# Issuing the query side's three spreads of keys and queries from ScalarE's queue instead of SyncE's

## What is computed

```python
# 64 samples of x and ctx (64 x 256 each); two samples make one pair
x = x + L0_xattn(layernorm(x), ctx)      # 8 heads of 8 channels, rotary positions on q and k:
    # q, k, v = Wq x + bq, Wk c + bk, Wv c + bv ;  q, k = rotary(q), rotary(k)
    # scores = q k^T / sqrt(8) ; p = softmax(scores) ; out = Wo (p v) + bo      (scores 256 x 256 a head)
x = x + L0_ffn(layernorm(x))             # three ternary linears, 256 -> 1024 -> 256, silu gate
x = x + L1_xattn(layernorm(x), ctx)      # one head over 64 memory rows, masked
x = x + L1_ffn(layernorm(x))             # bf16 ternary weights, silu gate, rms norm, 256 -> 1024 -> 256
```

## Time and profile before

| | us |
|---|---|
| median of 3 runs | 884.59 (882.81 to 884.67) |
| the profiled execution's own time | 885.19 |
| its span, first to last instruction | 883.4 |
| DVE busy | 744.9 (84%) |
| PE busy | 766.2 (87%) |
| ACT busy | 688.0 (78%) |
| POOL busy | 659.1 (75%) |

### The profile page before, as it was taken

One profiled execution on the slowest core, in us unless ns is written; L12 is line 12 of the kernel. 1 busy time (PEld: TensorE's weight loads), 2 busy tenths in 40 slices (PEclk: granted clock), 3 DMA queues, 4 the chain that ended last, 5 costly groups with the idle time before them and its releaser, 6 DMA issues. The chain is left out here.

```text
span 883.4 us, 21920 instructions
## 1 busy us (share of the span) xinstructions
PE 766.2 (87%) x6804; PEld 407.7 (46%) x6804; DVE 744.9 (84%) x1707; ACT 688.0 (78%) x1469; POOL 659.1 (75%) x1115
## 2 busy tenths in 40 slices
PE   0037878899999999999999999999999999998745
PEld 0023333444555555555555555555555554444422
DVE  0765778889999999999999999999999999966731
ACT  3655667779888888888888888888888889895531
POOL 5664435668888888888888888888888887677652
PEclk9995788889999999999999999999999999998986
DMA  9101122224444444444344444544444443345212
GB/s 338 11 13 55 38 64 57 78 72 103 104 109 108 104 109 104 101 114 103 101 101 104 107 109 109 110 107 105 109 109 105 104 102 98 90 85 108 68 46 71
DMA packets 210859, 84.67 MB, mean 96 GB/s; under 512 B 152748, under 2 KB 209708, under 8 KB 210744
## 3 DMA queue, kind: packets, MB, share of 16 engines
q1 hardware_dynamic: 210744, 83.28, 37.9%
HBM read 28.42 MB, written 4.72 MB: 38 GB/s over the span
## 5 line engine op out<-in xcount | busy, mean ns | idle before, releaser
L871 DVE TENSOR_REDUCE mx<-psS 128x2 f32<-128x512 f32 x512 | 338.2, 680 | 22.1 <-PE psS L435 21.4
L591 ACT ACTIVATE prob<-psT 128x512 f32<-128x512 f32 x512 | 293.8, 603 | 33.6 <-PE psT L443 32.6
L435 PE MATMUL psS<-KQ 31*128 31x256 f16 x1024 | 142.7, 283 | 23.5 <-DVE mx L871 21.5
L522 PE MATMUL psW<-guT,xT 128*128 128x512 bf16 x512 | 132.1, 393 | 15.8 <-DMA xT<-stage 13.1
L457 PE MATMUL psW<-prob,vst 128*32 128x256 f32 x2048 | 135.2, 394 | 0.1
L443 PE MATMUL psT<-KQ 32*128 32x256 f16 x1024 | 134.1, 278 | 1.0 <-ACT prob L591 0.5
L435 PEld LDWEIGHTS psS<-KQ 31*128 31x128 f16 x1024 | 42.1, 93 | 112.9 <-DVE mx L871 65.7
L777 POOL TENSOR_TENSOR stage<-stage 128x512 f16<-128x512 f32 x64 | 73.2, 1162 | 17.7 <-ACT stage L674 17.5
L457 PEld LDWEIGHTS psW<-prob,vst 128*32 128x32 f32 x2048 | 55.5, 111 | 60.5 <-issue 23.8
L484 PE MATMUL psW<-tern,xqT 128*128 128x512 bf16 x256 | 77.8, 386 | 4.0 <-DMA xqT<-xqB 3.6
L522 PEld LDWEIGHTS psW<-guT,xT 128*128 128x128 f16 x512 | 44.0, 100 | 76.9 <-issue 37.0
(11 more groups left out here) (163 smaller groups left out, 1772.8 us busy)
## 6 DMA issues: line engine op xcount, KB each, us to landing
KQ<-hl SPq DMA_DIRECT2D x192, 64.0 KB, 2.0
xP<-in_x SPq DMA_DIRECT2D x32, 128.0 KB, 2.2
cP<-in_ctx SPq DMA_DIRECT2D x32, 128.0 KB, 2.2
xA<-in_x SPq DMA_DIRECT2D x32, 128.0 KB, 2.5
oV<-uA SPq DMA_DIRECT2D x32, 128.0 KB, 2.2
oR<-rden_d SPq DMA_DIRECT2D x128, 32.0 KB
cB<-in_ctx SPq DMA_DIRECT2D x32, 128.0 KB, 2.3
out<-x SPq DMA_DIRECT2D x32, 128.0 KB, 1.8
```

Of the source, the lines that this page charges most:

```text
L435: m = nc.tensor.matmul(psS[:, n % 2, T * k:T * k + T], KQ[p % DEEP][r, 1, g, 128 * k:128 * k + 128], KQ[p % DEEP][r, 0, g, :], start=True, ...
L522: m = nc.tensor.matmul(bank, xT[:, NK * part + k, :], w[:, k, :], start=(k == 0 and part == 0), stop=(k == NK - 1 and part == 1))
L591: m = nc.scalar.activation(flat(prob[:, n % 8, :, :]), psT[:, n % 2, :], ACT.Exp, scale=float(HC) ** -0.5)
L871: m = nc.vector.tensor_reduce(mx[:, p % 2, :, 4 * (n % 4) + n // 4], psS[:, n % 2, :].rearrange("p (c s) -> p c s", c=NK), AX.X, ALU.max)
```

## The change

In ACT's row of `ORDER` a new step `kqa:1` stands behind `c1`, that is in the steady stretch behind `E10` and `pc` and ahead of `E11`. It issues the three transfers of the queries' side from ACT's queue; `kq` on SP keeps the three of the keys' side. Each has its own semaphore, and whoever waited for six transfers on `kq` waits for three on each. The sources, destinations, sizes and everything else are the same.

```diff
     "act": """...
-           E10:-1 pc:2 c1:28 E11:-1 tc4:1 E12:-1 mn:0 ...
+           E10:-1 pc:2 c1:28 kqa:1 E11:-1 tc4:1 E12:-1 mn:0 ...
@@ sp
                     elif name == "kq":
                         after_apart(sp, "lo", p)
                         after_apart(sp, "T", p - DEEP)
-                        for r, (k, q) in enumerate(((1, 2), (1, 3), (0, 2))):
-                            for side, part in enumerate((k, q)):
-                                sp.dma_start(KQ[p % DEEP][r::4, side, :, :], hl[:, part, :]).then_inc(S["kq"], 16)
+                        for r, part in enumerate((1, 1, 0)):
+                            sp.dma_start(KQ[p % DEEP][r::4, 0, :, :], hl[:, part, :]).then_inc(S["kq"], 16)
@@ pe, step S0
-                            after_dma(pe, "kq", p, 6)
+                            after_dma(pe, "kq", p, 3)
+                            after_dma(pe, "kqa", p, 3)
@@ act
+                    if kind == "kqa":
+                        after(act, "lo", p)
+                        after(act, "T", p - DEEP, NH - 1)
+                        for r, part in enumerate((2, 3, 2)):
+                            nc.scalar.dma_start(KQ[p % DEEP][r::4, 1, :, :], hl[:, part, :]).then_inc(S["kqa"], 16)
+                        continue
@@ act, step hi; the same on pool, step lo
-                        after_dma(act, "kq", p - 1, 6)
+                        after_dma(act, "kq", p - 1, 3)
+                        after_dma(act, "kqa", p - 1, 3)
```

More of the change, by code:

```diff
@@ L79 @@
     "act": """pTc:-5 xr:-3 hh1:-6 ab2:20 rn0:24 tc5:-4 E6:-1 E7:-1 xq:-3 sq0:-6 fr0:13 tc2:6 c0:37 E8:-1 u0:-1 E9:-1
-           E10:-1 pc:2 c1:28 E11:-1 tc4:1 E12:-1 mn:0 xh:-5 tB0:-3 tB1:-3 x1:-2 ab1:22 tc0:16 E13:-1 mxc:0 rn2:20
+           E10:-1 pc:2 c1:28 kqa:1 E11:-1 tc4:1 E12:-1 mn:0 xh:-5 tB0:-3 tB1:-3 x1:-2 ab1:22 tc0:16 E13:-1 mxc:0 rn2:20
            E14:-1 E15:-1 sq1:-6 hi:2 u1:-1 vst:2 E0:0 E1:0 th0:-5 xcTc:-4 tc1:8 E2:0 fr1:2 fr2:1 hr0:-3 E3:0 hr1:-3
@@ L771, in body @@
                         after(pool, "hi", p)
-                        after_dma(pool, "kq", p - 1, 6)
+                        after_dma(pool, "kq", p - 1, 3)
+                        after_dma(pool, "kqa", p - 1, 3)
                         m = nc.gpsimd.tensor_tensor(hl[:, 0::3, :], rot[:], hl[:, 1:3, :], ALU.subtract)
```

## The result

The changed kernel takes 909.39 us (median of 4 runs, 908.76 to 910.4) beside 884.63 us for the kernel before: the ratio is 1.0286, with a 95% interval of 1.0268 to 1.0303. It is 25 us slower, and outside the predicted range. The profiled execution took 909.59 us, 907.8 of it span.

What follows compares the result with a forecast made beforehand. DVE was taken as the bound, busy 21.94 of 22.60 us a period. From the profiled 885.19 us, -0.8 (start) + 0 + 0 gave 884.4, stated as 883.8 us against the median 884.59; range 881.0 to 894.

Steps and rivals of the forecast that it cites:

- What bounds the kernel: Steady period of 22.60 us: DVE is the bound, busy 21.94 us; ACT has 2.6 us of slack.
- SP's three issues: SP, steady stretch: losing three issues a pair frees 1.8 us, but nobody waits for SP, so the gain is 0.
- the place named for harm: ACT behind `pc`: late issues would delay `E11`, then `tB0` and `tB1`, then the second `aB` on DVE.
- The step that failed: ACT's steady stretch: its queue reads ahead by four or more, so three issues end by 411.1 or 411.6; cost 0.
- ends: ACT's three issues: cost 0 if its queue reads far ahead, 17 to 26 us if they start only after `pc`.
- Rival B: ACT's queue holds one instruction behind the running one, so part of the issue shows: 885 to 892 us, chance 0.17.
- The lateness absorbed: Between `E11` and the second `aB` on DVE: a lateness of 0.5 us is absorbed, DVE loses the rest.
- The 0.38 us wait before `x2`: DVE's wait for PE, 0.38 us a period: part of a lateness comes back there, since PE can catch up.
- -0.8: Start, `S0` of pair 0: earlier landing of transfers gains between 0 and 1.66 us; the middle, -0.8, was taken.
- rival C: The issue stops ACT, starting only after `pc`, and delays `S0` at the start by 1.6 us: 903 to 912, chance 0.15.
- the case in which both queues issue at once: Start, pair 0: ACT issues three beside SP's, the last landing at 71.95, so the whole 1.66 us wait goes.
- Rival D: Steady stretch: earlier transfers shorten the period itself, where DVE idles before `x2`: about 880.5 to 882.5 us, chance 0.10.

Runs made afterwards that it cites:

- The version from pair 7 on: The changed kernel, but pairs 0 to 6 have all six transfers on SP and `kqa` issues only from pair 7 on: 897.35 us, ratio 1.0145.
- `kqa` behind `E8`: The changed kernel with ACT's three issues behind `E8`, ahead of `u0`, instead of behind `pc`: 893.58 us, ratio 1.0118.
- `T10` ahead of `pc`: The changed kernel with ACT's three issues one place earlier, directly ahead of `pc` instead of behind it: 910.89 us, ratio 1.0302.
- `T3` behind `hr1`: The kernel before, all six transfers on SP, plus three idle issues on ACT behind `hr1` into a tile nobody reads: 890.64 us, ratio 1.0078.
- `E11` 2.07 us late: The changed kernel with five of the six transfers on ACT behind `pc` instead of three, one on SP: 967.21 us, ratio 1.0949.

## Why the prediction was wrong

**What bounds the kernel: right.** DVE is still the bound, with the new loss at its `aB`. That SP's three issues were worth nothing in the steady stretch held as well, and so did the place named for harm: `E11`, then `tB0`, then `aB`.

**The step that failed** is "It reads ahead by four or more. Then the issues are reached when `u0` starts, at 409.26, or earlier in the 1.38 us gap", taken at a cost of 0. Whatever the depth, no issue here went ahead of an instruction whose wait was unmet. Behind `pc`, which waits for PE's `proj1`, the issues cannot begin before `proj1` is done: in the steady stretch they do so at 427.63 with `pc` at 427.62; at 104.25 they do so 0.07 us ahead of `pc`. So they ended 0.05 us before `E11` started and made it 0.77 us late, which cost 0.57 us a period, where the sum had 0. The Trainium skill's figure of 8 entries ("Advanced Engine Details and Errata", Engine Queue Depths) is neither borne out nor refuted: no run here shows ACT's queue more than two instructions ahead, but each time an unmet wait held it there. I had chosen between ends by cover ("the gap of 1.38 us and the 2.3 us of queued work behind it are long beside 1.8 us") without asking whether the issues could get past `pc` at all, which stood directly ahead of them with a wait of its own.

**Rival B had the moment, not its reason, and not the size.** Its D of 0.65 to 0.8 us is the 0.77 measured, and its issues begin with the first `pc`. But it had them held by a queue of one, and the rows show two instructions ahead and an unmet wait. It made 0 to 8 us of its D, where two things went otherwise. The lateness absorbed was taken as 0.5 us; at `aB0` it was 0.40, and over the whole period 0.20. The 0.38 us wait before `x2` was to take up some; it stood unchanged at 0.37. So 25 x 0 to 0.3 became 24 x 0.57 = 14 us, and the 11 us of the start came on top.

**The start was worse than any case had it.** I gave it -0.8, with rival C at +1.6, and looked at pair 0 alone. `S0` of pair 0 came 0.55 us late, but pairs 1 to 3 lost 10 more: there `E11` has no slack before it and waits 2.2, 1.0 and 1.0 us for the issues in the rows (1.3 of the 2.2 through one held issue), PE's `T` with it, and the granted clock is lower. The version from pair 7 on returns 12 us. How these divide between the waits and the clock was not separated.

**Rival C's sum of 903 to 912 us holds the result by chance.** Its mechanism, issues that begin only after ACT has finished `pc`, with D = 1.55 (its own rows give 411.56 + 1.8 - 411.85 = 1.51), is not what the rows show; `pc` and the issues overlap. For the gain at the start, the case in which both queues issue at once was the true one: ACT's and SP's three issues ran beside each other in 2.16 and 1.88 us with `kqa` behind `E8`, not in turn. `pc` of pair 1 ahead of them kept the change from having it. Rival D did not show: the wait before `x2` stayed, and the steady period grew.

## What to carry to other kernels

A DMA issue is an instruction of its engine's queue of about 0.6 us: whatever stands behind it is held until it has ended, and it did not start here before every wait ahead of it was met. So place issues directly behind work that is queued and ready, and count the ready work between them and the next instruction with a deadline: here two issues fitted into 1.14 us of `pc`, and the third cost 0.57 us a period. Ask for the slack of the first instruction held back, its PSUM bank's next writer included, in the first iterations as well as in the steady ones. And leave issues on the engine that has idle time, since issues are held up now and then: 29 of the 704 issues from 60 to 800 us in the kernel before took over 0.3 us more than usual.

## What the runs showed of the hardware

- ACT's issues did not pass an unmet wait: the first one began 0.085 us after the semaphore of `proj1` behind `pc`, 0.085 after that of `T10` ahead of `pc`, and 0.116 after that of `T3` behind `hr1`, pair after pair. They ran ahead of two instructions that had not begun (409.28, with `E3` and `hr1` ahead); how deep the queue is was not shown.
- Two queues issue side by side: 0.54 us on ACT beside 0.59 on SP. The Trainium skill ("Perfetto Trace Analysis", DMA Instruction - HWDGE) has the descriptor block locked for one user. No run here shows issues in turn. Some sharing shows where both begin almost together: behind `E8` the second issue of ACT at the start, 0.04 us behind one of SP, took 0.84 us for 0.62. What both queues plainly shared were the holds, which mostly end within 0.02 us of each other.
- Fetches of 16 KB of instructions, 55 in a run, go with held issues: 26 of 83 near one, 3 of 621 elsewhere. That the fetch is the cause was read from the coincidence, and no kernel here took the fetches away.
- With `E11` 2.07 us late, eight of 21 steady periods had a stretch at the half clock level behind PE's wait: 26.10 us at a mean clock of 0.93 beside 24.47 at 1.00, same work. The kernel before and the changed one had none between 200 and 700 us.
